# Moving a transposition, a copy and the mixer's projections within the step of a fused Mamba and mixture-of-experts kernel, with two buffers for the weighted rows

## What is computed

```
xn = layernorm(x)
# mamba, for each batch of 512 tokens
x_ssm, x_gate = split(xn @ in_proj_w.T + in_proj_b)
x_conv = silu(causal_conv4(x_ssm) + conv_b)
Bm, Cm = split(x_conv @ bc_w.T + bc_b)              # 16 states each
dt = softplus(x_conv @ dt_w.T + dt_b)
h[t] = h[t-1] * exp(dt[t] * A) + dt[t] * Bm[t] * x_conv[t]
y[t] = sum_n h[t, :, n] * Cm[t, n] + x_conv[t] * D
z = (y * silu(x_gate)) @ out_w.T + out_b + xn
mamba = layernorm(z) * ln_g + ln_b
# experts: 8 experts, each token goes to the best 2
logits = silu(xn @ rw1 + rb1) @ rw2 + rb2
w = softmax over the two largest logits
experts = xn + sum_e w_e * (silu(xn @ we1[e] + be1[e]) @ we2[e] + be2[e])
```

## Time and profile before

| what | value |
|---|---|
| median of 3 runs | 942.38 us (940.24 to 944.92) |
| profiled execution | 942.98 us |
| its span in the profile | 940.8 us |
| PE busy | 793.0 us (84%) |
| DVE busy | 790.5 us (84%) |
| ACT busy | 664.5 us (71%) |
| POOL busy | 598.3 us (64%) |
| main part, first scan to last | 144.7 to 912.6 us |

### The profile page before, as it was taken

The page is one execution under the profiler, slowest core; times in us unless marked ns, Lnnn a source line. Parts: engine busy times, 40 slices in busy tenths (PEclk is TensorE's granted clock), DMA queues, the critical chain, the costliest instruction groups (busy, mean ns, idle before and its releaser), DMA issues.

```text
span 940.8 us, 14382 instructions
## 1 busy us (share of the span) xinstructions
PE 793.0 (84%) x4533; PEld 642.3 (68%) x4533; DVE 790.5 (84%) x774; ACT 664.5 (71%) x1134; POOL 598.3 (64%) x384
## 2 busy tenths in 40 slices
PE   3994649978998899989989899889988998899852
PEld 2662538757786778768876877687767786778742
DVE  7808818899889988997899798989899789979993
ACT  1433566877688768877796878876887689769930
POOL 3571413666578757777667757884777587758861
PEclk9995979999999999999999999999999999999985
DMA  9934096667666976697668865786678666977741
GB/s 299 384 141 156 8 367 236 208 201 226 204 197 216 263 215 195 206 261 241 219 178 249 253 221 158 229 268 202 201 203 261 212 209 204 267 214 228 234 89 23
DMA packets 81928, 201.02 MB, mean 214 GB/s; under 512 B 7936, under 2 KB 41216, under 8 KB 81728
## 3 DMA queue, kind: packets, MB, share of 16 engines
q1 hardware_dynamic: 61424, 171.46, 53.3%
q0 software_dynamic: 19168, 26.59, 15.0%
q10 hardware_dynamic: 1264, 2.05, 0.7%
HBM read 174.38 MB, written 26.61 MB: 214 GB/s over the span
## 4 chain that ended last, share of the span: by engine, by line
PE 33%; DVE 22%; ACT 9%; DMA 9%; issue 8%; POOL 2%; SPq 1%; DVEq 0%; ACTq 0%; POOLq 0%
PE ps_up L1237 15%; DVE ps_drive L941 9%; PE ps_yx L1251 8%; DVE ring L948 6%; PE ps_fr L1168 5%; DMA bc_scratch<-sp 5%; DVE ps_drive L934 5%; DMA out<-yo,sid 4%; ACT L792 3%; PE ps_up L1231 2%; ACT da L765 2%; PE ps_fr L1193 1%; DVE xx L915 1%; POOL y L597 1%; SPq L524 1%
## 5 line engine op out<-in xcount | busy, mean ns | idle before, releaser
L597 POOL TENSOR_TENSOR y<-y,ring 128x1024 f32<-128x1024 f32 x126 | 326.2, 2589 | 59.8 <-ACT y L756 51.9
L941 DVE TENSOR_TENSOR_SCAN ps_drive<-da,ps_drive 128x1024 f32<-128x1024 f32 x128 | 293.7, 2295 | 39.8 <-ACT da L765 36.0
L1237 PEld LDWEIGHTS ps_up<-xgt,w1s 128*128 128x128 f32 x2272 | 290.7, 200 | 18.8 <-issue 9.6
L1237 PE MATMUL ps_up<-xgt,w1s 128*128 128x128 f32 x2272 | 290.2, 283 | 0.0
L1251 PE MATMUL ps_yx<-w,ht 128*128 x1136 | 271.0, 382 | 0.0
L1251 PEld LDWEIGHTS ps_yx<-w,ht 128*128 128x128 f32 x1136 | 206.7, 192 | 28.9 <-issue 5.0
L586 POOL DMA_INDIRECT out<-yo,sid x71 | 115.7, 1629 | 144.8 <-ACT yo L807 86.4
L792 ACT ACT_TABLE_LOAD x143 | 183.5, 1283 | 2.6
L934 DVE TENSOR_TENSOR ps_drive<-ps_u,rep 128x1024 f32<-128x1024 f32 x128 | 157.4, 1229 | 15.9 <-DMA rep<-bc_scratch 6.5
L765 ACT ACTIVATE da<-gd,col 128x511 f32<-128x511 f32 x256 | 168.4, 710 | 0.0
L948 DVE TENSOR_TENSOR ring<-ps_drive,rep 128x1024 f32<-128x1024 f32 x128 | 156.5, 1223 | 3.9
(11 more groups left out here) (161 smaller groups left out, 724.7 us busy)
## 6 DMA issues: line engine op xcount, KB each, us to landing
w1s<-in_we SPq DMA_DIRECT2D x71, 1024.0 KB, 7.4
rep<-bc_scratch SPq DMA_DIRECT2D x128, 512.0 KB, 4.6
w<-in_we SPq DMA_DIRECT2D x8, 1024.0 KB, 10.0
w<-in_x SPq DMA_DIRECT2D x8, 512.0 KB, 11.1
xn_scratch<-da SPq DMA_DIRECT2D x8, 512.0 KB, 7.4
xnt_scratch<-xx SPq DMA_DIRECT2D x8, 512.0 KB, 5.2
out<-w POOLq DMA_DIRECT2D x8, 512.0 KB, 6.5
xx<-xnt_scratch SPq DMA_DIRECT2D x8, 512.0 KB, 3.5
```

The costliest lines, as they stand in the source:

```text
L597: pool.tensor_tensor(y[:, :, :], y[:, :, :], ring[:, g % RING, :, :], ALU.add).then_inc(s_sum, 1)
L941: dve.tensor_tensor_scan(states, da[:, g % DECAYS, :, :].rearrange("p k l -> p (k l)"), states, 0.0, ALU.mult, ALU.add).then_inc(s_scanned, 1)
L1237: mm = pe.matmul(bank[:, c * P:(c + 1) * P], w1s[:, q, k, at:at + P], xgt[:, k, :], start=False, stop=(c == 3 and k == KD - 1))
```

## The change

- PE: the second half of `up` follows at once on the first. The projections of the mixer that stood between the halves (`proj_out` of step 0, `proj_in`, `proj_bc`, one `proj_dt`) now stand behind both halves.
- PE: `turn_x(s + 2)` stood between the halves of `down`; it now stands right behind `up`, in front of the projections and of `down`.
- ACT: `copy_x(s + 2)` stood behind the Exp table; it now stands right behind the two `hidden`, in front of everything of the mixer that ACT does in that step.
- `yo` has two buffers; `weigh(j)` waits for scatter `j - 2` in place of `j - 1`. `scatter` itself still waits for the scatter before it.

```diff
@@ buffers
-        yo = sb("yo", [P, D])
+        yo = sb("yo", [P, 2, D])
@@ POOL, scatter
-                    pool.indirect_dma_start(out[:, :], bass.IndirectOffsetOnAxis(ap=sid[:, s:s + 1], axis=0), yo[:, :], None,
+                    pool.indirect_dma_start(out[:, :], bass.IndirectOffsetOnAxis(ap=sid[:, s:s + 1], axis=0), yo[:, s % 2, :], None,
@@ ACT, weigh
-                    if positive(j):
-                        act.wait_ge(s_scattered, j * 16)
-                    act.activation(yo[:, :], yx_y, ACT.Copy, scale=wslot[:, bass.ds(j, 1)]).then_inc(s_weighed, 1)
+                    if j > 1:
+                        act.wait_ge(s_scattered, (j - 1) * 16)
+                    act.activation(yo[:, j % 2, :], yx_y, ACT.Copy, scale=wslot[:, bass.ds(j, 1)]).then_inc(s_weighed, 1)
@@ ACT, step
                         for h in range(2):
                             hidden(s + 1, h)
+                    if s + 2 < MT:
+                        copy_x(s + 2)
                     if i in (0, 1):
                         gate_in(b, i, front["gate", b, i])
...
-                    if s + 2 < MT:
-                        copy_x(s + 2)
                     if i + 1 < IN:
                         decay(b, i + 1, 1)
@@ PE, step
                     if s + 1 < MT:
                         up(b, i + 1, e_next, 0)
+                    if s + 1 < MT:
+                        up(b, i + 1, e_next, 1)
+                    if s + 2 < MT:
+                        turn_x(s + 2)
+                    e_after = expert(s + 2) if s + 2 < MT else None
                     if i == 0 and b > 0:
                         proj_out(b - 1, 1)
...
-                    if s + 1 < MT:
-                        up(b, i + 1, e_next, 1)
-                    e_after = expert(s + 2) if s + 2 < MT else None
...
                     if s < MT:
                         down(s, e, 0)
-                        if s + 2 < MT:
-                            turn_x(s + 2)
                         down(s, e, 1)
```

## The result

The changed kernel takes **996.26 us** (median of 7 runs, 994.78 to 1005.61) where the kernel before took 943.85 us on the same chip (7 runs, 940.24 to 949.87): a ratio of **1.057, 95% interval 1.053 to 1.061**. The forecast was 952.6 with 940.5 to 961.0: the sign was right, and the loss of 53 us is five times the 10 that were worked out. The profiled execution took 1005.61 us, with a span of 1003.5.

What follows compares the result with a forecast made beforehand. Bound: a loop of tap, DVE's pace, B and C's store, then ACT and PE to the next tap. Batch 0's 0.85, six periods' 7.2 and the last boundary's 2.1 add 10.2, giving 952.6 us; range 940.5 to 961.

Steps and rivals of the forecast that it cites:

- What bounds the kernel: Tap-to-tap stretches and DVE's waits for decays (36.0 us) and first convolution product (20.8); order can give back 56.8 at most.
- only this last part can change: Of the loop from tap to tap, only the chain after B and C's store lands, through ACT and PE, can change.
- The boundary, 2.6 to 2.9 later: Step 7 into the next batch: waiting turn 0.95, clock 1.64, register load 0 to 0.3 delay DVE's scan.
- Step 0 gives back 1.44: Second half of `proj_out` no longer waits for DVE's addition, returning 1.44 us on average of the boundary's 2.6 to 2.9.
- DVE's 0.63: DVE's wait at its scan at 653.01, after the boundary; the decay comes early enough, so 0.63 us is regained.
- Both orders give the product at the same time: 6.4: Step 2's `proj_in`, 2.0 us later on PE, still gives its product after 6.4, so the tap gets only inherited lateness.
- Steps 3 to 6 have room: DVE does not wait there, and SP's loads go by DVE: Between tap and batch end the change costs nothing, since DVE has no waits and SP's loads follow DVE.
- The buffers 0: Two row buffers remove ACT's 12 scatter waits, 18.4 us, but these are off the path, so taken as 0.
- (a): Rival: PE's clock holds through the 4 us wait, or is back before `down`; 941 us, chance 0.14.
- (d): Rival: ACT's waits for the scatter count after all; up to 18.4 us less, 924; chance 0.05.
- (b): Rival: PE's clock stays low longer, 2.8 us lost at each boundary; 8 more, 961 us; chance 0.12.
- (c): Rival: step 7's transposition hardly waits, `down` fills PE's gap, a period is 3.4 us shorter; 920 us; chance 0.10.

Runs made afterwards that it cites:

- f4_step7: Changed kernel with, in step 7 alone, the transposition of the next tokens behind both halves of `down`; 977.3 us, 1.037 against the kernel before.
- g4_fill: Changed kernel with four unread matmuls added in step 7, in PE's gap ahead of the transposition; 990.1 us, 1.050 against the kernel before.
- h2_0: Changed kernel with the transposition of step 0 alone behind the output and gate projections; 998.6 us, 1.060 against the kernel before.
- h1_56: Changed kernel with the transposition of steps 5 and 6 behind `proj_bc` and the second `proj_dt`; 982.0 us, 1.043 against the kernel before.
- e1_rows: Kernel before with only the two buffers for the weighted rows (`yo`, `scatter`, `weigh`); 942.5 us, 0.998 against the kernel before.

## Why the prediction was wrong, step by step

1. **What bounds the kernel**: right as a frame; the loss is DVE's two waits (+75.9) less what its own instructions became shorter by (15.9). But "only this last part can change", the chain from the store of B and C to the next tap, was wrong: from the tap to `dt_in` of step 6 it was 45.1 to 46.2 before and is 50.4 to 52.6 in five of seven batches. The first stretch (+1.2 for 1.05 to 1.35) agrees by luck.
2. **The boundary, 2.6 to 2.9 later**: right in its mechanism and nearly in its size, 3.3 on average. The turn waits 3.79 in the first where 4 to 5 was said, and 1.96 to 2.3 in the others, where PE itself comes to it later; 1.95 in the first for the clock and the register load where 1.64 and up to 0.3 was said; f4_step7 takes 2.7 per boundary away again. The clock's share is about 1.0 per boundary (g4_fill, 6.9 over seven, uncertain as said).
3. **Step 0 gives back 1.44**: wrong. The wait of the output projection for DVE's sum was covered, but the same sum is needed again, for the bank of the gate's projection that now stands right behind: 8.8 us for 10.1. The step asked what L1190 waits for and not what the next projection on the same bank does. DVE's 0.63 became 0.36. h2_0 shows that step 0 has nothing more to give. With the 1.44 left out, the forecast's own sum would have been 8.6 higher, 961.
4. **"Both orders give the product at the same time: 6.4"**: wrong, and with step 5 the costliest. It is 6.42 before as was said, and 7.01 and 7.37 after. The register load, which the boundary's term counted, was left out here though it stands ahead of the projection too (0.41 and 0.25). In step 3 the transposition starts 4.69 behind `up`, for the 4.25 of the sum, and takes 0.41 for 0.2. By itself this is 0.6 at the tap and 0.95 of lateness on ACT and POOL.
5. **"Steps 3 to 6 have room: DVE does not wait there, and SP's loads go by DVE"**: wrong, the step that the forecast failed by. It was read from DVE alone. DVE did have room, but ACT's and POOL's lateness moves POOL's store towards SP's load, both slow down, the gather queued behind them lands in 11.6 instead of at most 7.7, and the transposition, which had half of `down` ahead of it before, is now the first to need it. The prices of moving the turn for its gather were never worked out, though every instruction that it waits for should have been. Steps 2 and 3 together: 27 us.
6. **Steps 5 and 6**: not priced either. `proj_bc` and `proj_dt` stand behind the turn; h1_56 gives 13 us.
7. **The buffers 0, the projections alone neutral**: right (-1.8 and -3.7). The advice of the Trainium skill ("Trainium Kernel Development and Optimization", Best Practices) to double-buffer for performance, which the prediction priced at 18.4 us and set aside, gained nothing that could be told here: e1_rows, 0.998 (0.994 to 1.002).
8. **The rivals**: (a) and (d) did not come. (b), 2.8 lost to the clock at the boundary, did not either: `down` behind the turn of step 7 took 4.8 to 5.4 in all seven, 1.1 to 1.8 over 3.62, near the 1.64 that was taken. The clock cost more at a place that no rival had, the projection behind the gather's wait (3.78 for 1.9). (c), the faster case, named the right place, the turn of step 7, and asked for the right thing, that it should not stand still there. No case combined two parts of the change, and none let the stretch from the tap to `dt_in` change; that is where the range failed: it was a sum of parts.

## What to carry to other kernels

An instruction that waits is priced by what stands behind it, on its own engine and by every engine that those release; so put a step that has two sources (here a SiLU and a gather) behind all work that has its inputs already, and not ahead of it because it is short. When several parts of a change touch one queue, work out their product too: here the projections alone won 4, the tokens lost 25, and the two lost 53. And a lag of 1 to 2 us on an engine with idle time is not free if it moves a transfer: list the transfers that hang on it and what they then meet.

## What the runs showed of the hardware

- A store of 512 KB that adds to memory, next to a load of 1024 KB issued on another queue behind it, at 114 places in the 19 profiles (six batches each): with the load 0.3 to 2.3 us behind it landed in 9.7 to 13.8 us (48 places), with 2.4 to 3.1 between in 7.2 to 10.5 (7), with 3.3 or more in 5.8 to 8.4 (59). An indirect gather issued 1.7 behind it on POOL's queue went with it: 8.8 to 12.5, 6.8 to 9.6, 5.2 to 8.4. The load itself went from 7.0 to 8.1 (before) up to 8.9 to 10.5 (after).
- After a wait of 1.96 us, 16 matmuls of `down` took 5.40 us instead of 3.62, the first 3 us of them at a granted clock of 0.51 (the lower of the two levels, 1.2 GHz in place of 2.4); with matmuls that nobody reads in that gap they took 3.62, at 1.00. After a wait of 0.5 (the row at 393.13) they took 3.62 too.
- In after, PE stands 0.20 to 0.52 us between the transposition and the next matmul at 41 of 69 places. Before, where no register load stands between them, there is no such gap at any of 69; that the gap is the register load is read from the order of the instructions.
